# Attention and FFN block, 32 batch elements on one core: two f16 parts for the projections' operands, and norms by two scalars per row on GpSimd

## What is computed

```python
xn = layernorm(x)                              # eps 1e-5
h  = xn * rsqrt(mean(xn**2) + eps) * norm_w    # RMS norm in the attention block
q, k, v = h @ Wq, h @ Wkv[:, :1024], h @ Wkv[:, 1024:]   # 16 heads of 64
q, k = [t / max(norm(t), 1e-12) * (gamma + 1) * 8 for t in (q, k)]  # per head
sim  = tanh(q @ k.T / 50) * 50 / 8
attn = softmax(sim) @ v @ Wo
m1, m2 = products of even and odd rows 1..16 of xn       # rank 4
ffn  = gelu(xn @ (W1 + scale*m1).T + b1) @ (W2 + scale*m2).T + b2
out  = x + attn + ffn
```

## Time and profile before

| what | value |
|---|---|
| time, median of 3 runs | 1054.89 us (1052.05 to 1056.09) |
| the profiled execution's own time | 1055.9 us |
| its span, first to last instruction | 1053.9 us |
| TensorE matmul busy | 1028.4 us, 98% |
| GpSimd busy | 978.2 us, 93% |
| ScalarE busy | 972.1 us, 92% |
| VectorE busy | 934.2 us, 89% |
| mean granted TensorE clock | 0.988 of full speed |

### The profile page before, as it was taken

How to read it: one execution, slowest core, us unless ns; L and a number is a source line. 1 busy time by engine, 2 the same in 40 slices (tenths; PEclk the granted TensorE clock), 3 DMA queues, 4 the chain that set the end, 5 groups by cost and what they waited for, 6 DMA issues and landing times.

```text
span 1053.9 us, 34270 instructions
## 1 busy us (share of the span) xinstructions
PE 1028.4 (98%) x12905; PEld 847.4 (80%) x12905; DVE 934.2 (89%) x2218; ACT 972.1 (92%) x1417; POOL 978.2 (93%) x912
## 2 busy tenths in 40 slices
PE   7699999999999999999999999999999999999997
PEld 5468888888888888888888888888888888888876
DVE  6989999999999999999999999999999999899972
ACT  4599999999999999999999999999999999999995
POOL 6799999999999999999999999999999999999873
PEclk7899999999999999999999999999999999999999
DMA  3344444444444435444445444344454445554351
GB/s 118 57 79 82 86 83 78 77 83 90 79 81 80 83 77 92 78 87 79 78 78 92 77 88 78 78 83 88 80 90 78 74 84 84 83 87 78 73 97 27
DMA packets 310491, 85.44 MB, mean 81 GB/s; under 512 B 282020, under 2 KB 309816, under 8 KB 310328
## 3 DMA queue, kind: packets, MB, share of 16 engines
q1 hardware_dynamic: 310328, 83.25, 43.6%
HBM read 11.09 MB, written 4.19 MB: 14 GB/s over the span
## 4 chain that ended last, share of the span: by engine, by line
PE 87%; ACT 5%; SPq 3%; issue 2%; DMA 2%; DVE 1%; POOL 0%; DVEq 0%; ACTq 0%
PE ps_scores L531 17%; PE ps_y L568 10%; PE ps_aux L446 9%; PE ps_aux L448 8%; PE ps_aux L447 8%; PE ps_o L557 7%; PE ps_o L559 5%; PE ps_aux L506 5%; PE ps_o L558 5%; PE ps_aux L517 5%; PE ps_y L567 5%; ACT clamped L654 1%; ACT probs L661 1%; PE ps_aux L512 1%; SPq L411 1%
## 5 line engine op out<-in xcount | busy, mean ns | idle before, releaser
L1073 POOL TENSOR_TENSOR probs_lo<-probs 128x1024 f16<-128x1024 f32 x256 | 484.8, 1894 | 19.4 <-ACT probs L661 19.2
L654 ACT ACTIVATE clamped<-ps_scores 128x1024 f32<-128x1024 f32 x256 | 265.6, 1037 | 41.2 <-PE ps_scores L531 35.9
L661 ACT ACTIVATE probs<-clamped 128x1024 f32<-128x1024 f32 x256 | 273.1, 1067 | 3.0 <-PE ps_o L559 0.4
L557 PEld LDWEIGHTS ps_o<-v_hi,probs 128*128 128x128 bf16 x2048 | 184.0, 98 | 55.3 <-issue 53.3
L531 PE MATMUL ps_scores<-heads_T 64*128 64x256 f16 x3072 | 212.1, 271 | 5.4 <-ACT clamped L654 3.8
L557 PE MATMUL ps_o<-v_hi,probs 128*128 128x65 bf16 x2048 | 214.8, 195 | 1.4 <-DVE ps_n L826 1.1
L558 PE MATMUL ps_o<-v_lo,probs 128*128 128x64 bf16 x2048 | 212.4, 193 | 0.0
L559 PE MATMUL ps_o<-v_hi,probs_lo 128*128 128x65 bf16 x2048 | 211.8, 194 | 0.0
L558 PEld LDWEIGHTS ps_o<-v_lo,probs 128*128 128x128 bf16 x2048 | 187.8, 99 | 0.0
L559 PEld LDWEIGHTS ps_o<-v_hi,probs_lo 128*128 128x128 f16 x2048 | 187.7, 97 | 0.0
L446 PE MATMUL ps_aux<-w_hi,xhT_hi 128*128 128x512 f32 x384 | 172.4, 449 | 8.5 <-DVE qk L876 5.7
(11 more groups left out here) (96 smaller groups left out, 1996.0 us busy)
## 6 DMA issues: line engine op xcount, KB each, us to landing
heads_T<-halves SPq DMA_TRANSPOSE x512, 2.5
x_in<-in_L_attn_tokens_dram SPq DMA_DIRECT2D x32, 128.0 KB, 2.4
x_res<-in_L_attn_tokens_dram SPq DMA_DIRECT2D x32, 128.0 KB, 2.3
out_dram<-y_sb SPq DMA_DIRECT2D x32, 128.0 KB, 2.0
sel_raw<-xn SPq DMA_DIRECT2D x192, 4.0 KB
qk<-in_L_attn_Wkv_dram SPq DMA_DIRECT2D x2, 512.0 KB, 5.2
qk<-in_L_attn_Wq_dram SPq DMA_DIRECT2D x1, 512.0 KB, 3.6
qk<-in_L_ffn_W_dram SPq DMA_DIRECT2D x2, 256.0 KB
```

The lines of the kernel that those rows point to most:

```text
L557: pe.matmul(full, hi[:, col], v_hi[:, par, u, h], start=(u == 0), stop=False)
L654: nc.scalar.activation(clamped[:].rearrange("p j n -> p (j n)"), ps_scores[:].rearrange("p j n -> p (j n)"), ACT.Tanh).then_inc(clamp_done, 1)
L661: nc.scalar.activation(probs[:, pair % RING].rearrange("p j n -> p (j n)"), clamped[:].rearrange("p j n -> p (j n)"), ACT.Exp, bias=LIFT, ...
L1073: g.tensor_tensor(probs_lo[:, buf].rearrange("p j n -> p (j n)"), probs[:, buf].rearrange("p j n -> p (j n)"), probs[:, buf].rearrange("p ...
```

## The change

1. The projections' operands (`w_hi`, `w_lo`, `xhT_hi`, `xhT_lo`) become f16. So that two f16 parts suffice, the weights are scaled by a factor computed at the start from `norm_w` and the weights' largest magnitudes: `weight_max`, `sum_bounds`, `weight_scale`. The scale falls out of q and k in their norms (the floor of the norm, `norm_floor`, is scaled with it), and for v it is taken back in the output weights `wo_sb`, on GpSimd, once.
2. `norm_apply` on GpSimd: each of the two outputs is made, 128 tokens at a time, by one instruction with the mean and the reciprocal deviation as two scalars per row. The intermediate `x_mid` and its semaphore go.
3. Slots 5 and 6 of TensorE's steps: one product of the result moves from slot 5 to slot 6 (4, 2 become 3, 3).
4. At the start the order of ScalarE's and VectorE's first tasks changes, and the copies of the transposed FFN weights come a step later.

```diff
-    [("scores",), ("values",), ("v", 0, 1), ("v", 1, 1), ("y", 4)],
-    [("scores",), ("values",), ("k", 0, 2), ("k", 1, 2), ("y", 2), ("v", 2, 1), ("v", 3, 1)],
+    [("scores",), ("values",), ("v", 0, 1), ("v", 1, 1), ("y", 3)],
+    [("scores",), ("values",), ("k", 0, 2), ("k", 1, 2), ("y", 3), ("v", 2, 1), ("v", 3, 1)],
...
-        w_hi = sb("w_hi", [P, QKV], F32R)
-        w_lo = sb("w_lo", [P, QKV], F32R)
+        w_hi = sb("w_hi", [P, QKV], F16)
+        w_lo = sb("w_lo", [P, QKV], F16)
...
-        x_mid = sb("x_mid", [P, TT, P])
-        xhT_hi = sb("xhT_hi", [P, 2, seq], F32R)
-        xhT_lo = sb("xhT_lo", [P, 2, seq], F32R)
+        xhT_hi = sb("xhT_hi", [P, 2, seq], F16)
+        xhT_lo = sb("xhT_lo", [P, 2, seq], F16)
...
+            def sum_bounds(i):
+
+                if i == 0:
+                    pe.wait_ge(nw_abs_made, 1)
+                    pe.wait_ge(w_max_made, 2)
+                    for c in range(2):
+                        ins = pe.matmul(ps_aux[:, 1, 0:1], nw_abs[:].to_broadcast([P, P]), w_max[:, c:c + 1],
+                                        start=(c == 0), stop=(c == 1))
+                else:
+                    pe.wait_ge(gammas_copied, 2)
+                    pe.wait_ge(w_max_made, 3)
+                    ins = pe.matmul(ps_n[:, 0:1], nw_abs[:].to_broadcast([P, P]), w_max[:, 2:3], start=True, stop=True)
+                ins.then_inc(w_summed, 1)
...
             def weights_hi(c):
                 part = slice(c * HEADS * DH, (c + 1) * HEADS * DH)
-                act.wait_ge(w_scaled, c + 1)
-                nc.scalar.copy(w_hi[:, part], w_raw[:, part]).then_inc(w_hi_made, 1)
+                i = c // 2
+                act.wait_ge(w_scale_made, i + 1)
+                nc.scalar.activation(w_hi[:, part], w_raw[:, part], ACT.Copy, scale=w_scale[:, i:i + 1])\
+                    .then_inc(w_hi_made, 1)
...
-            def scale_weights(c):
+            def weight_max(c):
                 dve.wait_ge(w_loaded[c], 32 if c == 0 else 16)
-                part = w_raw[:, c * HEADS * DH:(c + 1) * HEADS * DH]
-                v.tensor_scalar(part, part, nw_col[:, 0:1], None, ALU.mult).then_inc(w_scaled, 1)
+                v.tensor_reduce(w_max[:, c:c + 1], w_raw[:, c * HEADS * DH:(c + 1) * HEADS * DH], AX_X, ALU.max,
+                                apply_absolute_value=True).then_inc(w_max_made, 1)
+                if c == 0:
+                    v.tensor_reduce(nw_abs[:], nw_col[:], AX_X, ALU.max, apply_absolute_value=True).then_inc(nw_abs_made, 1)
+
+            def weight_scale(i):
+
+                dve.wait_ge(w_summed, i + 1)
+                one = slice(i, i + 1)
+                v.tensor_scalar(w_bound[:, one], ps_aux[:, 1, 0:1] if i == 0 else ps_n[:, 0:1], BOUND_MIN, BOUND_MAX,
+                                ALU.max, ALU.min).then_inc(w_bounded, 1)
+                dve.wait_ge(w_bounded, i + 1)
+                v.reciprocal(inv_bound[:, one], w_bound[:, one]).then_inc(w_inverted, 1)
+                dve.wait_ge(w_inverted, i + 1)
+                v.tensor_scalar(w_scale[:, one], nw_col[:], inv_bound[:, one], WEIGHT_TOP, ALU.mult, ALU.mult)\
+                    .then_inc(w_scale_made, 1)
...
-            scale_weights(0)
-            scale_weights(1)
+            weight_max(0)
+            weight_max(1)
+            weight_scale(0)
+            aux(first, *XT_TASK[1:])
             weights_lo(0)
             weights_lo(1)
-            aux(first, *XT_TASK[1:])
-            scale_weights(2)
+            weight_max(2)
...
-                g.tensor_tensor(x_mid[:], x_in[:, par], mean_var[:, :, 0:1].to_broadcast([P, TT, P]), ALU.subtract)\
-                    .then_inc(mid_made, 1)
-                pool.wait_ge(mid_made, b + 1)
-                g.tensor_tensor(xn[:, par], x_mid[:], rstd[:, 0].unsqueeze(2).to_broadcast([P, TT, P]), ALU.mult)
-                g.tensor_tensor(xh[:], x_mid[:], rstd[:, 1].unsqueeze(2).to_broadcast([P, TT, P]), ALU.mult)\
-                    .then_inc(xn_made, 1)
+                for a, o in ((0, xn[:, par]), (1, xh[:])):
+                    for t in range(TT):
+                        ins = g.tensor_scalar(o[:, t], x_in[:, par, t], mean_var[:, t, 0:1], rstd[:, a, t:t + 1],
+                                              ALU.subtract, ALU.mult)
+                ins.then_inc(xn_made, 1)
...
+                        pool.wait_ge(consts_loaded, 16 * 3)
+                        pool.wait_ge(w_bounded, 2)
+                        flat = wo_sb[:].rearrange("p q n -> p (q n)")
+                        g.tensor_scalar(flat, flat, w_bound[:, 1:2], 1.0 / WEIGHT_TOP, ALU.mult, ALU.mult)\
+                            .then_inc(wo_scaled, 1)
```

More of the change, by code:

```diff
@@ L42 @@
 NORM2_MIN = 1e-24
+WEIGHT_TOP = 2.0 ** 15
+BOUND_MIN, BOUND_MAX = 2.0 ** -40, 2.0 ** 100
 RSQRT_SEED = float(0x5F3759DF - (1 << 22) - (1 << 30))
@@ L176, in block_kernel @@
         nw_col = sb("nw_col", [P, 1])
+        nw_abs = sb("nw_abs", [P, 1])
+        w_max = sb("w_max", [P, 3])
+        w_bound = sb("w_bound", [P, 2])
+        inv_bound = sb("inv_bound", [P, 2])
+        w_scale = sb("w_scale", [P, 2])
+        norm_floor = sb("norm_floor", [P, 1])
         g_bc = sb("g_bc", [P, HEADS * DH])
@@ L253, in block_kernel @@
         rows_loaded = sem("rows_loaded")
-        w_scaled = sem("w_scaled")
+        nw_abs_made = sem("nw_abs_made")
+        w_max_made = sem("w_max_made")
+        w_summed = sem("w_summed")
+        w_bounded = sem("w_bounded")
+        w_inverted = sem("w_inverted")
+        w_scale_made = sem("w_scale_made")
+        norm_floor_made = sem("norm_floor_made")
+        wo_scaled = sem("wo_scaled")
         w_hi_made = sem("w_hi_made")
@@ L269, in block_kernel @@
         xn_made = sem("xn_made")
-        mid_made = sem("mid_made")
         q_squared = sem("q_squared")
@@ L618, in run @@
                     pe.wait_ge(consts_loaded, 16 * 3)
+                    pe.wait_ge(wo_scaled, 1)
                 if st.number == batches:
@@ L623, in run @@
                 for s in range(PAIRS):
+                    if st.number == -2 and s == 6:
+                        sum_bounds(1)
                     for what, *k in TENSOR_STEPS[s]:
@@ L642, in _ @@
             aux(first, *XT_TASK)
+            sum_bounds(0)
             keep_busy(2)
@@ L703, in run @@
                 if st.number == -1:
+                    ffn_copies()
                     act.wait_ge(ffn_copied, 3)
                 for s in range(PAIRS):
-                    if st.number == -2 and s == 5:
+                    if st.number == -2 and s == 7:
                         weights_hi(2)
-                    if st.number == -2 and s == 7:
-                        ffn_copies()
                     for what, *k in SCALAR_STEPS[s]:
@@ L740, in _ @@
                 nc.scalar.copy(g_bc[:, j * 512:(j + 1) * 512], (ps_y, ps_n)[j][:]).then_inc(gammas_copied, 1)
+            aux(Step(-1, 0, ()), *XT_TASK[1:])
+            weights_hi(0)
+            weights_hi(1)
             run_all(act, run)
@@ L766, in xT_lo @@
                 dve.wait_ge(xnT_copied, b + 1)
-                v.tensor_tensor(xhT_lo[:, par], bank[:, 0:seq], xhT_hi[:, par].bitcast(F32), ALU.subtract).then_inc(xT_split, 1)
+                v.tensor_tensor(xhT_lo[:, par], bank[:, 0:seq], xhT_hi[:, par], ALU.subtract).then_inc(xT_split, 1)
             def sum_squares(st, k, ahead):
@@ L786, in seed @@
                     wait(dve, newton_step, 9 * b)
-                    v.tensor_scalar(minus_half_norm2, norm2[:], NORM2_MIN, -0.5, ALU.max, ALU.mult)\
+                    dve.wait_ge(norm_floor_made, 1)
+                    v.tensor_scalar(minus_half_norm2, norm2[:], norm_floor[:, 0:1], -0.5, ALU.max, ALU.mult)\
                         .then_inc(seed_made, 1)
@@ L915, in run @@
                     if st.number == -2 and s == 6:
+                        weight_scale(1)
+                    if st.number == -2 and s == 7:
                         weights_lo(2)
```

11 lines of the change are left out of this document (6 added, 5 removed).

## The result

The changed kernel takes 1087.91 us (median of 6 runs, 1087.19 to 1088.23) against 1054.86 us for the kernel before in the same job: the ratio is 1.0314, 95% interval 1.0301 to 1.0327. It is slower by 33 us, where 23 us of gain were forecast.

A forecast was written before the change was run, and what follows sets the result against it. TensorE bounds the 31.43 us period, the others mostly following. 28 periods x 0.81 = 22.7 us, plus 1.3 in periods on both sides, less 0.7 at the start: 23.3 off, 1032 us against 1054.9; range 1023 to 1047.

The forecast's parts named there:

- TensorE's part: On TensorE, 36 projection matmuls per period become f16: 0.50 us plus 0.40 at group starts, 0.90 us saved, leaving 30.53.
- the slow group starts: On TensorE, five projection groups per period whose first matmul takes 0.31 us, 0.08 more than its neighbours; f16 saves 0.40.
- the outcome that the prediction drew from this: On TensorE, weight load already hidden behind 512 columns: the 0.50 us falls away, 0.40 left, period 31.03; rival, chance 0.20.
- GpSimd's part: Norms on GpSimd: four instructions at 0.30 us each replace three products of 0.61, saving 0.63; GpSimd needs 30.2 us.
- The rival that this was: Slower: scalars from memory are dear on GpSimd; from 0.61 us each it decides; 1103 us at 1.03; chance 0.09.
- The sign of being wrong that the prediction gave: Wrong if TensorE's bank waits exceed 0.4 us a period, a GpSimd instruction 0.5 us, or the start's delay 1.5 us.
- How the three meet: TensorE 30.53, ScalarE 30.36, GpSimd 30.2 us together: period between 30.53 and 30.71, taken as 30.62, 0.81 less than now.
- ScalarE alone would need 31.43 - 1.07: ScalarE's waits for scores, 0.39 and 0.68 us a period, counted as room, so it needs 30.36 us.
- The move of the product: One f32 result product from TensorE's slot 5 to 6: scores of slot 6 0.22 us sooner, counted as nothing.
- The start: Before the first projection, new maxima and weight scale replace three scalings: +0.7 us, between 0 and 1.5.
- Only the group starts gain: TensorE's f16 matmul still costs 0.23 us or bank handover eats the gain; period 31.03, 1044 us; chance 0.20.
- No change: ScalarE's waits are traded for TensorE's for banks and heads, 0.8 us a period; 1053 to 1056 us; chance 0.08.

The follow-up runs named there:

- e10: The changed kernel with the four GpSimd norm instructions adding the mean instead of subtracting it (output changed): 1050.8 us, period 31.20 us.
- e1: The changed kernel with the norms on GpSimd applied by the old three tensor products, f16 and the rest kept: 1052.3 us, ratio 0.9969.
- e8: e1 with the first of the three products, the subtraction of the mean, left out: 1048.2 us, period 31.20 us.
- e12: e1 with the copy of k's first quarter ahead of the exponential in ScalarE's slot 6: 1051.2 us, ratio 0.9965.
- e3: e1 with the result's product also moved back from slot 6 to slot 5: 1053.0 us, ratio 0.9970.
- e2: The kernel before with only the new two-scalar norm instructions on GpSimd, f32 operands kept: 1089.1 us, ratio 1.0318.
- e11: e8 with the copy of k's first quarter ahead of the exponential in ScalarE's slot 6: 1040.9 us, period 30.92 us.
- e6: The changed kernel with the four two-scalar norm instructions moved from GpSimd to the end of VectorE's slot 6: 1110.0 us, ratio 1.0522.
- e13: e12 with the bias b2 added by f16 matmuls on TensorE instead of by GpSimd, residual loaded later: 1061.2 us, ratio 1.0062.
- e14: The kernel before, f32 operands kept, with the early copy of k and the bias b2 added by TensorE: 1075.0 us, ratio 1.0193.
- e15: e13 with the bias added by one full-height f32 product per 128 tokens instead of f16 matmul pairs: 1054.5 us, ratio 0.9991.

## Why the prediction was wrong

**TensorE's part: right.** Distance 0.216 us (0.220 taken, 0.216 as bound), the slow group starts gone, 1.05 us in place of 0.90. The Trainium skill (TensorE: Matmul & The Clock Gate, Weight-path perf modes) says of fast weight load that it wins where the free dimension is small; the outcome that the prediction drew from this, nothing saved behind 512 columns, did not come: 0.234 became 0.216. Whether the weight load or the stream of the reduced format cost those 0.018 us, no run separates.

**GpSimd's part: the step that failed first.** "I take 0.30, since it is the same kind of work as the cast." Measured: 0.80. The interval of 0.30 to 0.42 rested on rows that share the shape and not the operation, and the subtraction alone costs 0.355 us of the 0.80 (e10). The rival that this was, with its point of decision at 0.61 us, was the case that came (chance 0.09). Its formula gives 30.83 - 1.83 + 4 x 0.80 = 32.2 and 0.77 x 28 = 22 us. 33 came: the period is 32.52, because the queue is bound into circle B and keeps its wait for the probabilities (0.32 x 28 = 9 us more), and the start is 2 us later. The sign of being wrong that the prediction gave, an instruction over 0.5 us, came, and so did the other two: TensorE's waits for banks over 0.4 us a period, and a start later by more than 1.5 us.

**How the three meet: failed as well, on its own.** With the GpSimd part undone the forecast would have been 1032 us; e1 gives 1052.3. The failed step is to take each engine's waits as room: "ScalarE alone would need 31.43 - 1.07", GpSimd 31.43 - 0.60, and "VectorE has 2.6 us free in a period, which I leave out as a bound". ScalarE's wait of 0.68 us for the scores of slot 3 is 0.68 in the kernel before, in the changed one and in e1, and GpSimd's 0.22 for the probabilities stays 0.21: these are hand-overs of a circle, not room. VectorE's free time lies ahead of slot 7; from its first reciprocal there to q's last multiplication it has none. The bound is the longer of two circles over three or four engines, 31.21 us (A: e1, e8, e10) and 31.20 (B: e12, and every run whose edit lies on it). Busy sums per period can't show either. On A lie three of the 36 projection matmuls and on B none; in the kernel before A stood 0.13 us below the period, it became 0.09 shorter itself, and so TensorE could pass on 0.22 of its 1.05.

**The move of the product:** nothing, right (e3). **The start:** the first marker comes at 55.91 us where it was 53.90, +2.0 us, and outside the stated 0 to 1.5. With the norms undone it comes at 52.84 (e1) and 53.72 (e3), with the new norms alone at 56.68 (e2): the delay is the norms', and no cost of the new preparation of the weights is seen, against +0.7 taken.

**Rivals.** "Only the group starts gain" and "No change" named TensorE's waits for banks, the right place; "No change" asked for 0.8 us of new waits per period, and e1 has 0.83.

## What to carry to other kernels

Price a new instruction by a row with the same operation, not the same shape; where there is none, the dear bound has to come from the dearest row of that engine, and on an engine with 0.6 us of reserve per period this alone decides the sign. When four in-order engines stand at 89 to 98%, the next bound is not the engine with the next largest busy sum but a circle over the dense stretches of several: find it by following one engine's queue from each hand-over to the next until the period closes, before pricing a gain. Count a hand-over only where the receiver stood idle for it; the chain view named one at 215.44 that was none. A wait that an engine has before the change is room only if it lies on no such circle. And two bounds at the same height hide each other: only cutting both (e11) showed either.

## What was not expected of the hardware

- GpSimd, subtract and multiply with scalars from memory, f32: 0.80 us for 128 elements a row, 1.23 for 256; with one scalar constant 0.72 for 128; add and multiply 0.445; multiply and multiply by one scalar from memory and a constant 1.12 us for 1,024. That the operation and not the operands sets it is shown for subtract against add in this form; two tensors subtracted take 0.61 us for 256 elements, like two multiplied. Why, no run shows.
- VectorE's two-scalar instruction on 128 elements from and to SBUF takes 0.335 us, but 0.96 and 1.08 us while GpSimd's squares of k run beside it (e6, same run; near the start, with GpSimd idle, all four take 0.335). That one engine holds the other off is argued from the times of start and end, not tested by itself.
- A pair of f16 matmuls of one row and 128 columns between full-height ones costs 0.41 us with its neighbours' slower starts, 0.81 us for two pairs (e13, e14), more than one f32 product of full height in place of each pair (0.22 us, e15).
